# Message sums of a graph network in four column tiles of 32 nodes, with wide one-hot operations

## The reference

```
xn  = layernorm(x)
agg = segment_sum((xn @ w_gnn)[src] * edge_weight[:, None], dst)
x   = x + relu(agg) + linear_attention(xn) @ wo.T + bo
h   = layernorm(x)
for _ in range(30):
    h = h + 0.01 * tanh(h)
    h = h * sigmoid(h)
    h = layernorm(h) * ln_w + ln_b
    h = h @ W.T + b
out = x + h
```

## Time and profile before

| what | value |
|---|---|
| median of 3 runs | 4113.03 us (4112.46 to 4115.05) |
| profiled execution, first to last instruction | 4114.6 us |
| busy TensorE, VectorE, ScalarE, GpSimd | 3911.4, 3767.4, 3440.1, 3204.4 us |
| granted TensorE clock, mean | 0.996 |
| set-up, until the first gather | 100.4 us |
| early stage, until about | 565 us |
| gathers | 1666 |
| last gather | 3450.4 us |

### The profile page before, as it was taken

How to read it: one execution, slowest core, us unless ns; L and a number is a source line. 1 busy time by engine, 2 the same in 40 slices (tenths; PEclk the granted TensorE clock), 3 DMA queues, 4 the chain that set the end, 5 groups by cost and what they waited for, 6 DMA issues and landing times.

```text
span 4114.6 us, 83954 instructions
## 1 busy us (share of the span) xinstructions
PE 3911.4 (95%) x29240; PEld 3681.5 (89%) x29240; DVE 3767.4 (92%) x7281; ACT 3440.1 (84%) x5133; POOL 3204.4 (78%) x3823
## 2 busy tenths in 40 slices
PE   0899989999999999999999999999999999999999
PEld 0788879999998999999999999999999999899999
DVE  6888779999999999999999999999999999999998
ACT  3333278888888999999899999989999999999998
POOL 4677788888888888888888888888888886555555
PEclk9999999999999999999999999999999999999999
DMA  8555322222223222222322222233222221100000
GB/s 303 163 159 153 110 84 81 77 79 81 77 81 98 82 80 80 76 80 81 99 80 80 75 81 82 75 95 89 75 81 80 76 81 52 52 1 1 1 2 26
DMA packets 215405, 340.39 MB, mean 83 GB/s; under 512 B 79160, under 2 KB 152502, under 8 KB 214994
## 3 DMA queue, kind: packets, MB, share of 16 engines
q0 software_dynamic: 80768, 219.99, 18.7%
q1 hardware_dynamic: 120126, 83.28, 6.9%
...
## 4 chain that ended last, share of the span: by engine, by line
PE 52%; DVE 30%; ACT 9%; POOL 5%; issue 3%; DMA 1%; ACTq 0%; DVEq 0%; SPq 0%; POOLq 0%
PE MM L1439 27%; PE TR L1431 11%; PE AGG L1347 9%; DVE st L1161 7%; DVE v_low L1201 6%; DVE T L1186 6%; ACT T L760 3%; DVE hot L1069 3%; POOL gat_even L562 2%; PE XB L1359 2%; ACT v_high L774 2%; ACT T L765 2%; DVE ve L1166 2%; DVE k_n L1101 1%; POOL rs L536 1%
## 5 line engine op out<-in xcount | busy, mean ns | idle before, releaser
L562 POOL DMA_INDIRECT gat_even<-xn_d,src_cur x1496 | 1495.8, 1000 | 395.7 <-issue 356.2
L1439 PE MATMUL MM<-w_high,v_high 128*128 128x256 f32 x5880 | 1708.4, 291 | 0.0
L1439 PE MATMUL MM<-w_high,v_low 128*128 128x256 f32 x5880 | 1645.5, 280 | 0.0
L1439 PE MATMUL MM<-w_low,v_high 128*128 128x256 f32 x5880 | 1645.2, 280 | 0.0
L1439 PEld LDWEIGHTS MM<-w_low,v_high 128*128 128x128 f32 x5880 | 1114.0, 189 | 0.0
L1439 PEld LDWEIGHTS MM<-w_high,v_high 128*128 128x128 f32 x5880 | 1111.3, 189 | 0.0
L1439 PEld LDWEIGHTS MM<-w_high,v_low 128*128 128x128 f32 x5880 | 1107.1, 188 | 0.0
L765 ACT ACTIVATE T<-T,sh,rs 128x256 f32<-128x256 f32 x2072 | 1093.8, 592 | 2.8 <-DVE sh L1171 2.8
L1161 DVE BATCH_NORM_STATS2 st<-T 128x6 f32<-128x512 f32 x1470 | 968.8, 700 | 124.8 <-ACT T L760 112.3
L774 ACT ACTIVATE v_high<-TR 128x1024 fp32r<-128x1024 f32 (+1 forms) x750 | 757.8, 1010 | 207.6 <-PE TR L1431 197.8
L1201 DVE SCALAR_TENSOR_TENSOR v_low<-TR,v_high 128x1024 fp32r<-128x1024 f32 (+1 forms) x750 | 896.2, 1195 | 25.8 <-ACT v_high L774 24.6
...
## 6 DMA issues: line engine op xcount, KB each, us to landing
gat_even<-xn_d,src_cur POOLq DMA_INDIRECT x1496, 2.8
...
```

The lines of the kernel that those rows point to most:

```text
L562: pool.indirect_dma_start(gat[gathered_in(j)][c][:], None, xn_d, bass.IndirectOffsetOnAxis(ap=src_cur[j % 2][:, c:c + 1], axis=0)).then_in ...
L1439: last = mm(MM[b][0:R, t // 2, t % 2 * D:(t % 2 + 1) * D], rows_, w, start=k == 0, stop=k == len(products) - 1)
```

## The change

- Edges are laid out on the host so that a chunk is 128 neighbouring edges: `src_laid`, `dst_laid` and `ew_laid` hold [128 partitions, 1582 columns] twice, the second time shifted by one column, and a window begins at the tile's first edge exactly. A partition still reads 17 neighbouring words.
- Since edges are sorted, 32 nodes (a side) need only some chunks. Side j is taken from chunks 4j-1 to 4j+4, six (`DEEP`); with chunk -1 left out these are 23 products of 32 columns, each into its own 32 partitions of the bank (`pairs_of`, `BURSTS`).
- The products of a tile are issued in four bursts of 7, 8, 4 and 4 (`g_burst`), sides changing from one product to the next. A burst waits once for its gathers, and only its last product counts (`bursts_multiplied`). Chunks are gathered in the order 3, 7, 11, 15, 0, 4, 8, 12, 16, 1, 5, ...; how many a slot is as before. The bursts stand in slots 3, 5, 7, 9 for the first tile and 11, 13, 0, 1 for the second.
- The 17 one-hot operations become two of 128 x 768 (`g_hot`): compare, then multiply by the weights, into one of two buffers. They stand in slots 1 and 9, the scalars in slots 0 and 8. In the early stage both stand in the step of the tile's first chunk.
- Whether each side's edges lie in its six chunks is checked in set-up: `range_ends` computes six probe positions for each tile, GpSimd gathers six single destinations, and `ranges_probe` compares them and adds to the count that `ok_col` is made from. `weights_kv` moves from group 13 to 12, the probe to 14, `range_starts` from 11 to 15.

The core of the diff:

```diff
-HOT_LAG, MUL_LAG = 1, 2
+MUL_LAG = 2
+SCALARS_AT, HOT_AT = (0, 8), (1, 9)
+GROUPS = [[c for c in range(KC) if c % SPAN == k] for k in (SPAN - 1, *range(SPAN - 1))]
+def pairs_of(g):
+    return [(d, j, SPAN * j - 1 + d) for d in range(DEEP) for j in range(SIDES) if SPAN * j - 1 + d in GROUPS[g]]
...
-                off = sp.value_load(off_row[0:1, j:j + 1], min_val=0, max_val=E - CAP)
-                for t, a in ((src_cur, src), (dst_cur, dst), (w_cur, ew)):
-                    sp.dma_start(t[e][:], a[bass.ds(off, CAP)].rearrange("(p k) -> p k", k=KC)).then_inc(S(f"edges_loaded{e}"), 16)
+                off = sp.value_load(off_row[0:1, j:j + 1], min_val=0, max_val=128 * LAID - 1)
+                for t, a in ((src_cur, src_laid), (dst_cur, dst_laid), (w_cur, ew_laid)):
+                    sp.dma_start(t[e][:], a[bass.ds(off, 128 * LAID)].rearrange("(p k) -> p k", k=LAID)[:, 0:KC]).then_inc(S(f"edges_loaded{e}"), 16)
...
+                if g == PROBES_AT:
+                    pool.wait_ge(S("probes_ready"), 1)
+                    for k in range(PROBES):
+                        pool.indirect_dma_start(q_dst[0:TILES, k:k + 1], None, dst.unsqueeze(1),
+                                                bass.IndirectOffsetOnAxis(ap=q_i[0:TILES, k:k + 1], axis=0)).then_inc(S("probes_gathered"), 16)
...
-                v.tensor_scalar(hot[c][:], iota_f[:], d_loc[:, c:c + 1], w_loc[:, c:c + 1], ALU.is_equal, ALU.mult).then_inc(S("hot_ready"), 1)
+                v.tensor_tensor(hot[e][:], by_pair(d_loc), iota_f[:].rearrange("p (j w) -> p j w", w=WIDE).unsqueeze(2).broadcast_to([128, SIDES, DEEP, WIDE]),
+                                ALU.is_equal).then_inc(S("hot_marked"), 1)
+                dve.wait_ge(S("hot_marked"), j + 1)
+                v.tensor_tensor(hot[e][:], hot[e][:], by_pair(w_loc), ALU.mult).then_inc(S("hot_ready"), 1)
...
-                mm(messages(j), hot[c][:], gat[gathered_in(j)][c][:], start=c == 0, stop=c == KC - 1).then_inc(S("chunks_multiplied"), 1)
+                for d, side, c in BURSTS[g]:
+                    last = mm(messages(j)[side * WIDE:(side + 1) * WIDE], hot[j % 2][:, side, d, :], gat[gathered_in(j)][c][:],
+                              start=(g, d) == FIRST_OF[side], stop=(g, d) == LAST_OF[side])
+                last.then_inc(S("bursts_multiplied"), 1)
```

More of the change, by code:

```diff
@@ L20 @@
 CAP = KC * 128
+WIDE = 32
+SIDES = R // WIDE
+SPAN = KC // SIDES
+DEEP = SPAN + 2
+LAID = -(-(E + CAP + 256) // 128)
+PAST = 1 << 20
+assert SIDES * WIDE == R and SPAN * SIDES + 1 == KC
 QUADS = 5
@@ L59, in grouped @@
     return [list(range(sum(counts[:k]), sum(counts[:k + 1]))) for k in range(len(counts))]
+GROUPS = [[c for c in range(KC) if c % SPAN == k] for k in (SPAN - 1, *range(SPAN - 1))]
+ORDER = [c for group in GROUPS for c in group]
+GROUP_OF = [g for g, group in enumerate(GROUPS) for c in group]
+def pairs_of(g):
+    return [(d, j, SPAN * j - 1 + d) for d in range(DEEP) for j in range(SIDES) if SPAN * j - 1 + d in GROUPS[g]]
+BURSTS = [pairs_of(g) for g in range(len(GROUPS))]
+FIRST_OF = {j: min((g, d) for g, burst in enumerate(BURSTS) for d, i, c in burst if i == j) for j in range(SIDES)}
+LAST_OF = {j: max((g, d) for g, burst in enumerate(BURSTS) for d, i, c in burst if i == j) for j in range(SIDES)}
+GROUP_ENDS = [max(i for i in range(KC) if GROUP_OF[i] == g) for g in range(len(GROUPS))]
+assert sum(map(len, BURSTS)) == SIDES * DEEP - 1
 LEAD = 6
@@ L88, in early_chunks, with early_bursts @@
     return [divmod(i, KC) for i in range(max(0, (step - LEAD) * PER_STEP), min(limit, (step - LEAD + 1) * PER_STEP))]
+def early_bursts(step):
+    return [(j, GROUP_OF[i]) for j, i in early_chunks(step, MUL_EARLY) if i in GROUP_ENDS]
 def last_step(tile):
@@ L115 @@
 FIND_AT, RANGES_AT = 5, 10
+PROBES_AT = RANGES_AT + 2
+PROBES = 2 * (SIDES - 1)
 X_AT = (0, 6)
@@ L266, in build @@
         w_cur = [sb(f"w_cur{e}", [128, KC]) for e in range(2)]
-        d_loc = sb("d_loc", [128, KC])
-        w_loc = sb("w_loc", [128, KC])
+        d_loc = sb("d_loc", [128, KC + 1])
+        w_loc = sb("w_loc", [128, KC + 1])
         gat = {name: [sb(f"gat_{name}{c}", [128, D]) for c in range(KC)] for name in ("even", "odd")}
-        hot = [sb(f"hot{c}", [128, R]) for c in range(KC)]
+        hot = [sb(f"hot{e}", [128, SIDES, DEEP, WIDE]) for e in range(2)]
         g_x = sb("g_x", [128, D])
@@ L1503, in _ @@
                     f_transpose(0, 0)
-                for j, c in early_chunks(s, MUL_EARLY):
-                    g_chunk(j, c)
+                for j, g in early_bursts(s):
+                    g_burst(j, g)
                 if s < K_TILES:
```

163 lines of the change are left out of this document (95 added, 68 removed).

## The result

The changed kernel takes **4138.36 us** (4135.73 to 4142.62, 4 runs), the kernel before beside it 4114.03 (4112.46 to 4115.05): ratio 1.006, 95% interval 1.0045 to 1.0074. It is slower by 0.6%, and the interval leaves no room for no change. Forecast were 4075 us, in a range of 4025 to 4130, with 0.7 on faster. The profiled execution spans 4140.8 us (before 4114.6).

The account below looks back on a forecast made before the run. TensorE bounds rounds 1 to 3, GpSimd right behind at 73.1 us a trip; rounds 1 to 3 -37.5, round 0 -8, set-up +7, together -38.5 from 4113.03, give 4075 us, range 4025 to 4130.

Parts of the forecast that it names:

- TensorE, narrow products: Products of 32 columns: half a full chunk, 0.216 us each, so TensorE needs 4.8 us less a trip.
- rival 1: Column tiles on TensorE do not overlap, 0.43 us a product; 4396 us, chance 0.14.
- Mode switches: TensorE changing kind of matmul: 16 switches a trip at 0.08 us each, 1.3 us; other bound 0.16 each, 2.6 us.
- It saves 3.2 us a tile: VectorE's two wide operations replacing 17 one-hot ones: 6.4 us less a trip, worth nothing by itself.
- the sum's excess of 0.9 us over the floor: Trip time above GpSimd's own time after the change: 74.0 us a trip in rounds 1 to 3, -37.5 us in all.
- round 0's 1.7: Round 0 before the change: a trip takes 71.4 us against GpSimd's floor of 69.7, an excess of 1.7.
- The floor of 73.1: GpSimd's time a trip in rounds 1 to 3 without waits for other engines; a trip can shrink by 2.2 us.
- The early stage: First 20 tiles, gathering beside the attention sums: GpSimd's 1.25 us a gather stays, so the change is 0.
- Rival 4: Wide operations come as a lump in slots 1 and 9, GpSimd waits at the power behind; 4148 us, chance 0.06.
- Set-up: Range and probe steps added before the first gather: +7 us, bounds +2 and +12.
- Signs: Wrong if a burst spans over 2.4 us, gathers take under 0.9, or GpSimd waits long right after wide operations.
- GpSimd's waits for VectorE's variance fall from 62 us to near 25: Expected sign of the forecast in rounds 1 to 3: GpSimd waits less for VectorE's variance.

Follow-up runs that it names:

- e2: The changed kernel with five full fp32 products that nobody reads behind slot 10's products of each trip, filling TensorE's wait; 4098.8 us.
- e1: The changed kernel with its two wide one-hot operations of a tile cut into four pairs, spread over more slots; 4075.0 us.

## Why the prediction was wrong

- **TensorE, narrow products.** Taken as 0.216 us, half a chunk; measured 0.108 inside a burst, a quarter, and 0.15 with head and tail. Four column tiles ran side by side, and rival 1 is out. By the Trainium skill (TensorEngine Tiling (Array Packing), Key Properties) tiles operate independently; these bursts agree. My reason for a half was that the two records of one product share columns. Inside a burst records start 0.054 us apart on the mean, so that sharing did not set the pace; that products of other columns fill the gap is an inference.
- **Mode switches.** Priced 0.08 us each, bounds to 0.16. In slot 9 the burst's first record starts 0.21 behind the last product where others start 0.12 behind. Going out, the transposes start 0.31 behind the burst's last record. Less the 0.12 of ordinary products that is 0.28 us a burst, 2.2 a trip, inside the bounds. No run tells how much of it is the change of kind.
- **VectorE.** Wide operations measured 0.95 and 0.96 (forecast 0.94). "It saves 3.2 us a tile" was right, and it was worth less than nothing by itself, because what had stood spread over 15 slots stood in two.
- **The step that failed** is the sum's excess of 0.9 us over the floor. It was taken from an average, round 0's 1.7 halved because both engines would have room on the mean. Measured in rounds 1 to 3 are 75.4 - 72.9 = 2.5 us, more than the 2.2 before. The room was there, but not in the slot that the chain passed: slot 9 had the pair, the next input's statistics and the shift in one row. The runs showed in its place TensorE's wait of 2.68 us once a trip and the stretch at half clock behind it, worth 40 us (e2), and 66 us of the rounds with the pair cut in four (e1). With the pair cut in four the excess is 0.1 to 0.2 us, and the kernel takes 4075.0, the number that was forecast for the uncut pair. That agreement is partly luck: the early stage (+5 where 0 stood) and round 0 (trip 71.9 where 70.6 stood) cancel with a better trip of rounds 1 to 3 (73.4 where 74.0 stood).
- **GpSimd's floor.** The floor of 73.1 held in rounds 1 to 3 (72.9) and failed in round 0 (69.9 to 71.5). There the pair in slot 9 does meet a gather as it begins, and that gather took 1.72 to 1.77 us instead of 0.95 in each of the ten trips. The early stage was put at 0 and cost 6.4 us; its 1.25 us a gather was a reading of one place, for 339 intervals in 450.3 us are 1.33 each before. The step treated a GpSimd operation's duration as its own. It depends on what VectorE runs when it begins. The Trainium skill (GPSIMD Engine Reference, Specifications) says that GpSimd's SBUF interfaces are shared with VectorE, with contention against VectorE instructions in a two-port mode or with two SBUF inputs. The rows agree for two inputs, and the statistics with one input hold nothing up. The `tensor_scalar` of one input does, and it ran 768 elements in 0.61 us where two inputs took 0.95; that this is the two-port mode is likely by it, but no row names the mode. The rule was at hand, would have spoken against this change, and I did not weigh it.
- **Rival 4** had the slot, the mechanism's start and nearly the time (4148), at a chance of 0.06. It was off in what pays. GpSimd waits for the variance 60.4 us in rounds 1 to 3, 2.1 us a trip, near the 1.9 it gave. But 43.8 were there before, so this grew by 17 us only, and the longer wait is not at the power behind the pair, as the rival has it, but 15 us later, behind the half clock. The half clock, worth 40 us, the rival did not have; that its time came near is luck.
- **Set-up.** +7 forecast, +6.9 measured; the first gather came at 107.35.
- **Signs.** Of those named for being wrong, bursts over 2.4 us and gathers under 0.9 did not come; the third, long waits right after the wide operations, came for TensorE, and for GpSimd only 15 us later. "GpSimd's waits for VectorE's variance fall from 62 us to near 25" began with a misreading: 62 were all its waits, 43.8 the variance's. They rose to 60.4.

Open: why round 0 keeps its stretches at half clock with the pair cut in four (9 of them, in 10 trips), and how its 8.6 us more split. With the gap filled, and 2 stretches instead of 8, 3.3 of them came back (724.8 us), with the pair cut in four 6.1 (722.0); no run undid the hold alone.
